# Sums of a graph network's SUM and REL rounds: one-hot products added to a resident accumulator, in place of scans, stored states and gathers

## The chip, the cores and the metric

One core of one Trainium2 chip runs the whole network in one launch. The metric is the time of one execution on the device in microseconds, lower is better.

## The reference

A network of 3125 nodes with 64 features and 103125 edges sorted by destination is computed in seven rounds over all edges. The two rounds that matter here, with layer norms between, are these (cut):

```python
# SUM
norm = deg_inv[from_] * deg_inv[to_]
out = segment_sum(norm[:, None] * x[from_], to_, n)
x = layernorm(x + out)
# two attention rounds (ATT) and a skip layer, then
# REL
transformed = einsum('nd,rdo->nro', h, weight)      # 16 relations
msg = transformed[src, rel_type] * norm             # norm = edge_weight1
x = layernorm(x + relu(segment_sum(msg, dst, n)))
# three edge convolutions with a segment maximum (MAX) follow
```

## The kernel before

The edges, padded, are cut into 808 tiles of 128 (P), and four tiles (TC) make a step: 202 steps in SUM, ATT and REL, 101 double steps in MAX. `ROUNDS` is SUM, ATT, ATT, REL, MAX, MAX, MAX. Each engine has its own instruction stream, and `chunks` writes a round's loop for it: a list of stages, each with a lag in steps, is run in that order for every step. A ring of U = 4 slots (2U in DVE's and SP's loop here) holds rows, indices and results. Semaphores of a round (`idx_ready`, `rows_ready`, `turned`, `st_ready`, `back`, `hb_ready`) count steps.

A step of SUM or REL runs like this. ACT copies four columns of source indices into `idx` (L1150; in SUM also four columns of node numbers, L1142). POOL issues four indirect gathers, each of 128 rows of 64 floats (L1086), into `rows` (shown as edges_a); it waits for `idx` and for `turned` of four steps before. In REL DVE multiplies the rows by the edges' weights (L1580). PE's `turn` (L1309) transposes the four tiles, so that features lie on partitions and 512 edges along the free axis. DVE's `scan` (L1562) runs along these 512 columns, from the value carried over of the last step: state = near x state + value, where `near` is 1 if an edge has the same destination as the one before it. PE's `back` (L1406) transposes the states again, ACT copies them out of PSUM (`states_out`, L1163, into hb) and stores them to DRAM (`store_states`, L1236, the table states_sum). The last edge of each node then holds that node's sum. SP fetches the near flags with `fetch_batch` (four steps at a time), in SUM also the destination numbers. SUM does more beside it, for later rounds: DVE makes one-hots of the destinations (`make_onehots`, L1569), SP stores them, PE turns the edge features (`turn_edges`, L1300), and ACT copies (`edges_back`, L1169) and SP stores them.

At the round's end POOL gathers the last state of every node, 25 gathers of 128 nodes (L1114), into `agg`, and the node phase goes over the nodes in six groups of four blocks and one last block: DVE's `scaled` in SUM (L822) or `related` in REL (L842) read `agg`, layer norms follow, PE turns the new x (L668) and multiplies it (L675), ACT and DVE split the products (L484 to L505), and SP stores the tables that the next round gathers from. The order of each engine's node steps is written out by hand (`STEPS`, `groups`).

Ahead of the rounds a preamble computes on DVE (L1439 to L1550) the degrees, block tables and the flags `tile_same` from the destinations of each tile (`tile_dst`), and SP stores the flags (L938, L940) and the first source table (L943). `first_i` holds each tile's first destination; ATT and MAX rounds load windows of 128 nodes from it (`fetch_windows`, L409 on).

## Time and profile before

| | us |
|---|---|
| median of 3 runs | 9922.08 |
| lowest, highest | 9895.71, 9936.42 |
| profiled execution, its span | 9918.4 |
| SUM: gathers from 64, last scan at 1282, ATT's gathers from about 1345 | |
| ATT, two rounds | about 1345 to 4560 |
| REL: gathers from 4722, last scan at 5927, MAX's gathers from 5980 | |
| MAX, three rounds | 5980 to about 9880 |

All times in the rows are of that one execution, counted from its span's start. PE is TensorE's matmul side, PEld its weight load, DVE VectorE, ACT ScalarE, POOL GpSimd, SP SyncE; SPq is SP's queue as it issues DMAs. "PEclk" is the granted TensorE clock as a share of 2.4 GHz. "<-" in square brackets names what ended an idle time; "remote" is a signal whose sender the profile does not name, "issue" is idle time with no wait that it shows.

### The profile page before, as it was taken

To read this page: it belongs to the slowest core of one execution; us is meant where nothing else is said; L and a number is where in the kernel's file an instruction comes from. 1 tells how busy PE (TensorE), PEld (TensorE's weight loads), DVE (VectorE), ACT (ScalarE), POOL (GpSimd) and SP (SyncE) were. 2 spreads that over 40 slices of the span, in tenths; PEclk is the share of its full clock that TensorE was granted. 3 is DMA by queue.
4 is the path that set the end of the run, shared out by engine and by line. 5 is a ranking of instruction groups with operands and counts; after the bars stand their busy time and mean duration, and the time that the engine had idled before them with its cause. 6 is when DMAs were issued, how large, how long until landed. Compare 5 with 4: busy or idle time off the path is not lost.

```text
span 9918.4 us, 123616 instructions
## 1 busy us (share of the span) xinstructions
PE 3937.1 (40%) x24024; PEld 2674.1 (27%) x24024; DVE 2471.0 (25%) x4351; ACT 2035.1 (21%) x6406; POOL 5554.5 (56%) x5874
## 2 busy tenths in 40 slices
PE   2333334443343433336222224444444444444443
PEld 1222223333342333334111112222222222222222
DVE  4333333333332333332222221111111111111112
ACT  1111123333332333333101111111111111111111
POOL 6666644454434444442666665666656666556665
PEclk9999995555555555555555555666656666566666
DMA  4444434454444444443222223333333333333333
GB/s 121 126 126 126 125 91 108 109 110 107 108 92 97 109 106 107 107 107 99 54 50 50 51 48 82 91 90 90 89 79 90 90 90 90 80 89 90 91 91 80
DMA packets 2188624, 925.94 MB, mean 93 GB/s; under 512 B 1608302, under 2 KB 2071734, under 8 KB 2182134
## 3 DMA queue, kind: packets, MB, share of 16 engines
q1 hardware_dynamic: 1080022, 458.65, 19.0%
q10 hardware_dynamic: 921120, 272.38, 11.7%
q0 software_dynamic: 187392, 193.93, 9.6%
q8 instruction: 30, 0.49, 0.0%
q14 instruction: 60, 0.49, 0.0%
HBM read 657.48 MB, written 266.58 MB: 93 GB/s over the span
## 4 chain that ended last, share of the span: by engine, by line
issue 30%; PE 20%; another core or an unknown queue 9%; SPq 7%; DVE 2%; DVEq 1%; ACT 1%; DMA 0%; ACTq 0%; POOL 0%; POOLq 0%
PE ps L1323 7%; PE ps L1398 5%; PE ps L1319 3%; SPq L1002 3%; PE ps L1406 2%; PE ps L675 1%; PE ps L1309 1%; DVEq L374 1%; SPq L996 1%; SPq L1004 1%; SPq L998 1%; DVE edges_a L1580 1%; DVE st L1562 0%; SPq L370 0%
## 5 line engine op out<-in xcount | busy, mean ns | idle before, releaser
L1086 POOL DMA_INDIRECT edges_a<-src_table,idx x4040 | 3829.6, 948 | 2501.2 <-issue 1163.6
L1093 POOL DMA_INDIRECT edges_a<-src_table,idx x1616 | 1524.7, 944 | 1626.7 <-ACT weighted L1209 1063.1
L1323 PE MATMUL ps<-sel,win_sb 128*64 128x128 fp8e4 x7272 | 749.7, 262 | 1704.9 <-issue 1703.6
L1562 DVE TENSOR_TENSOR_SCAN st<-pen,st,ps 128x512 f32<-128x512 f32 x300 | 384.0, 1280 | 3279.9 <-remote 2939.6
L1406 PE MATMUL ps<-ident,st 64*128 64x64 f32 (+2 forms) x4444 | 849.1, 339 | 655.0 <-DVE st L1562 333.8
L1406 PEld LDWEIGHTS ps<-ident,st 64*128 64x128 f32 (+2 forms) x4444 | 705.6, 207 | 1063.1 <-issue 1039.8
L1323 PEld LDWEIGHTS ps<-sel,win_sb 128*64 128x64 bf16 x7272 | 396.2, 126 | 2056.6 <-issue 2009.9
L1562 DVE TENSOR_TENSOR_SCAN st<-edges_a,st,ps 64x512 f32<-64x512 fp8e4 x402 | 510.5, 1270 | 1665.6 <-remote 1292.0
L1309 PE MATMUL ps<-ident,edges_a 128*64 128x128 f32 x1616 | 421.4, 416 | 985.2 <-DVE edges_a L1580 643.5
L1335 PE MATMUL ps<-win_sb,sel 128*128 128x97 bf16 x4848 | 473.8, 271 | 849.1 <-issue 771.5
L1163 ACT ACTIVATE hb<-ps 128x256 f32<-128x256 f32 (+1 forms) x808 | 348.4, 431 | 2000.1 <-remote 1082.1
L1390 PE MATMUL ps<-ident,weighted 128*97 128x128 f32 x1616 | 452.8, 433 | 615.9 <-issue 279.9
L1595 DVE TENSOR_TENSOR prod<-ps,edges_a 128x388 f32<-128x388 f32 x404 | 225.4, 558 | 1795.3 <-remote 1459.7
L1335 PEld LDWEIGHTS ps<-win_sb,sel 128*128 128x128 fp8e4 x4848 | 396.1, 135 | 909.9 <-issue 826.0
L1319 PE MATMUL ps<-ident,edges_a 128*128 128x128 f32 x1212 | 439.2, 362 | 425.3 <-issue 354.7
L1227 ACT ACTIVATE edges_a<-ps,b 128x512 f32<-128x512 f32 x303 | 208.2, 687 | 1658.0 <-remote 1498.9
L1390 PEld LDWEIGHTS ps<-ident,weighted 128*97 128x97 f32 x1616 | 337.5, 274 | 659.9 <-issue 640.2
L1562 DVE TENSOR_TENSOR_SCAN st<-decay,st,ps 97x512 f32<-97x512 f32 x402 | 511.5, 1272 | 10.4 <-PE ps L1406 10.4
L1309 PEld LDWEIGHTS ps<-ident,edges_a 128*64 128x64 f32 x1616 | 216.4, 158 | 1063.7 <-issue 996.2
L1161 ACT ACTIVATE hb<-ps 128x512 f32<-128x512 f32 x303 | 180.9, 597 | 1555.4 <-issue 1386.1
L1398 PE MATMUL ps<-edges_a,w 128*128 128x512 f32 x606 | 481.9, 887 | 9.7 <-issue 8.0
L1209 ACT ACTIVATE weighted<-edges_a,weight 128x97 f32<-128x97 f32 x1616 | 471.9, 364 | 33.3 <-ACT hb L1163 23.9
(203 smaller groups left out, 3440.4 us busy)
## 6 DMA issues: line engine op xcount, KB each, us to landing
states_sum<-hb ACTq DMA_DIRECT2D x1010, 128.0 KB
win_sb<-dst_table SPq DMA_DIRECT2D x1616, 72.8 KB
edges_a<-src_table,idx POOLq DMA_INDIRECT x5656
states_att<-hb ACTq DMA_DIRECT2D x404, 194.0 KB
win_sb<-dst_table ACTq DMA_DIRECT2D x1212, 48.0 KB
win_sb<-dst_table SPq DMA_DIRECT2D x1212, 48.0 KB
dst_b<-in_dst_row SPq DMA_DIRECT2D x50, 1024.0 KB
sel<-onehots SPq DMA_DIRECT2D x303, 128.0 KB
```

The costliest lines, as they stand in the source:

```text
L1086: pool.indirect_dma_start(rows[:, s, j * D:(j + 1) * D], None, srcs[q.r], bass.IndirectOffsetOnAxis(ap=idx[:, s, j:j + 1], axis=0))\
L1093: pool.indirect_dma_start(xe_a[:, s, j * KA:j * KA + D], None, srcs[q.r], bass.IndirectOffsetOnAxis(ap=idx_a[:, s, j:j + 1], axis=0))\
L1163: nc.scalar.activation(hb[:, v, 0:TC * kw], bank(BACK, s)[:, 0:TC * kw], ACT.Copy)\
L1209: last = nc.scalar.activation(weighted[:, s % V, j * KA:(j + 1) * KA], xe_a[:, s, j * KA:(j + 1) * KA], ACT.Copy, scale=weight[:, gs_, o + ...
L1309: last = nc.tensor.matmul(bank(TURNED, s)[0:D, j * P:(j + 1) * P], rows[:, s, j * D:(j + 1) * D], ident[:, :], is_transpose=True, start=Tr ...
L1319: nc.tensor.matmul(bank(TURNED, s)[:, at_j], rows[:, s, j * P:(j + 1) * P], ident[:, :], is_transpose=True, start=True, stop=False)
L1323: last = nc.tensor.matmul(bank(TURNED, s)[h * D:h * D + D, at_j], win_pair(s, j, h)[:, i * D:(i + 1) * D], sel[:, s, h * EC + j * P:h * EC ...
L1335: last = nc.tensor.matmul(bank(TURNED, s)[:, j * KA:(j + 1) * KA], sel[:, v, j * P:(j + 1) * P], win_att(v, j)[:, i * KA:(i + 1) * KA], st ...
L1390: last = nc.tensor.matmul(bank(QUERY, s)[0:KA, j * P:(j + 1) * P], weighted[:, s % V, j * KA:(j + 1) * KA], ident[:, :], is_transpose=True ...
L1398: nc.tensor.matmul(bank(QUERY, s), w2[:, q.r - 4, :], xe[:, s, :], start=True, stop=True).then_inc(q.lifted.sem, 1)
L1406: last = nc.tensor.matmul(bank(BACK, s)[:, j * w:(j + 1) * w], st[0:w, s % V, j * P:(j + 1) * P], ident[0:w, 0:w], is_transpose=True, star ...
L1562: nc.vector.tensor_tensor_scan(st[0:w, s % V, :], d0, d1, init, op0, op1).then_inc(q.st_ready.sem, 1)
```

## The change

Rounds of the kinds in `WINDOWED`, SUM and REL, no longer scan, transpose back, store or gather states. As the destinations are sorted, the 128 edges of a tile reach into a window of at most 128 nodes, from the tile's first destination on. `slot`, made once in the preamble, holds for every edge its destination less the first one of its tile. In each step DVE makes one-hots `xe` from it (`spread_edges`: in SUM one instruction for four tiles, in REL four that carry the edge's weight as well and replace L1580); PE multiplies rows by one-hots (`window_sums`: four plain float32 matmuls of 128 columns in place of four transposes) into PSUM; and one step later DVE adds the four windows of 64 x 128 into a resident accumulator `acc` of 64 x 3328 at the column that a register gives (`add_windows`). POOL's gathers wait for `summed` in place of `turned`. In the node phase PE transposes `acc` by groups (`turn_sums`, after the last add), and `scaled` and `related` read PSUM in place of `agg`; POOL's 25 gathers are left out there. ACT's `states_out` and `store_states`, SP's near flags of SUM and all of SP's fetches of REL go. The one-hots and the edge features of SUM stay. The preamble gets seven transposes, three DVE instructions and an iota for `slot` and `ramp` (0 to 127), and SP clears two stretches of 6144 rows of the state table that MAX reads, ahead of the flags' stores. `acc` is `agg` under another name, `slot` is the former `mask`.

```diff
+WINDOWED = (SUM, REL)
...
-    self.turned = shared("turned", C_)
-    self.st_ready = shared("st_ready", C_)
-    self.back = shared("back", C_)
-    self.hb_ready = shared("hb_ready", C_)
-    if kind in (SUM, REL):
-        self.batch_ready = [shared(f"batch_ready_{h}", 16 * (1 + (kind == SUM)) * len(range(h * U, C, 2 * U)))
-                            for h in range(2)]
+    if kind in WINDOWED:
+        self.spread = shared("spread", C_)
+        self.summed = shared("summed", C_)
+        self.added = shared("added", TC * C_)
+    else:
+        self.turned = shared("turned", C_)
+        self.st_ready = shared("st_ready", C_)
+        self.back = shared("back", C_)
+        self.hb_ready = shared("hb_ready", C_)
     if kind == SUM:
+        self.batch_ready = [shared(f"batch_ready_{h}", 16 * len(range(h * U, C, 2 * U))) for h in range(2)]
         self.sel_made = shared("sel_made", C_)
         self.nodes_ready = shared("nodes_ready", C_)
-    if kind == REL:
-        self.weighted = shared("weighted", C_)
...
+def turn_sums(g):
+    b, nb = GROUPS[g]
+    wait(pe, (q.added, TC * q.steps))
+    if g >= V:
+        wait(pe, dve_did(q, g - V, "scaled" if r == 0 else "added"))
+    for j in range(nb):
+        last = nc.tensor.matmul(bank(SCORE, g)[:, j * D:(j + 1) * D], acc[0:D, (b + j) * P:(b + j + 1) * P],
+                                ident[0:D, 0:D], is_transpose=True, start=True, stop=True)
+    last.then_inc(q.pe.sem, 1)
...
-    dve.wait_ge(agg_ready[g], 16 * nb * (r + 1))
-    op(g, "scaled", nc.vector.tensor_tensor(y, a_g, wide(dinv[:, b:b + nb], D), ALU.mult))
+    wait(dve, pe_did(q, g, "turn_sums"))
+    op(g, "scaled", nc.vector.tensor_tensor(y, blocks_of(bank(SCORE, g), nb, D), wide(dinv[:, b:b + nb], D), ALU.mult))
...
+for end in (CH * EC, EP):
+    sp.dma_start(states[0][end - LATE_CHUNKS * EC:end, :].rearrange("(p n) f -> p n f", p=P),
+                 zrow[:, :].bitcast(f32)[:, 0:D].unsqueeze(1).to_broadcast([P, LATE_CHUNKS * TC, D]))\
+        .then_inc(tails_cleared, 16)
...
-        if k == SUM:
-            wait(sp, (q.sel_made, c - U))
-            e = slice(c * EC, (c + m) * EC) if isinstance(c, int) else bass.ds(c * EC, m * EC)
-            sp.dma_start(dst_b[:, of_slots, :].rearrange("p u e -> p (u e)"),
-                         dst_row[:, e].to_broadcast([P, m * EC])).then_inc(q.batch_ready[h].sem, 16)
-        wait(sp, (q.st_ready, c - U))
-        sp.dma_start(near[:, of_slots, :].bitcast(u8).rearrange("p u e -> p (u e)"),
-                     flags[of, :].rearrange("(o u) e -> o (u e)", o=1).to_broadcast([D, m * EC]))\
-            .then_inc(q.batch_ready[h].sem, 16)
+        wait(sp, (q.sel_made, c - U))
+        e = slice(c * EC, (c + m) * EC) if isinstance(c, int) else bass.ds(c * EC, m * EC)
+        sp.dma_start(dst_b[:, of_slots, :].rearrange("p u e -> p (u e)"),
+                     dst_row[:, e].to_broadcast([P, m * EC])).then_inc(q.batch_ready[h].sem, 16)
...
-        wait(sp, *tables_stored(q))
+        if k != REL:
+            wait(sp, *tables_stored(q))
-    elif k == REL:
-        chunks(sp, q.steps, (0, fetch_batch), ring=2 * U)
...
-        wait(pool, *sources_stored(q), (q.idx_ready, c + 1), (q.turned, c - U + 1))
+        wait(pool, *sources_stored(q), (q.idx_ready, c + 1),
+             (q.summed if q.kind in WINDOWED else q.turned, c - U + 1))
...
+    if q.kind in WINDOWED:
+        continue
...
-        chunks(act, q.steps, (0, indices), *[(U, edges_back)] * (k == SUM), (U + 1, states_out),
-               (U + 2, store_states))
+        chunks(act, q.steps, (0, indices), *[(U, edges_back)] * (k == SUM))
...
-    def turn(c, s, n):
-        made = [(q.weighted, c + 1)] if k == REL else []
-        wait(pe, (q.rows_ready[s], 64 * (n + 1)), *made, (q.st_ready, c - V + 1))
+    def window_sums(c, s, n):
+        wait(pe, (q.rows_ready[s], 64 * (n + 1)), (q.spread, c + 1), (q.added, TC * (c - U + 1)))
         for j in range(TC):
-            last = nc.tensor.matmul(bank(TURNED, s)[0:D, j * P:(j + 1) * P], rows[:, s, j * D:(j + 1) * D],
-                                    ident[:, :], is_transpose=True, start=True, stop=True)
-        last.then_inc(q.turned.sem, 1)
+            at_j = slice(j * P, (j + 1) * P)
+            last = nc.tensor.matmul(window_ps(s)[:, at_j], rows[:, s, j * D:(j + 1) * D], xe[:, s, at_j],
+                                    start=True, stop=True)
+        last.then_inc(q.summed.sem, 1)
...
-        chunks(pe, q.steps, *[(0, turn_edges)] * (k == SUM), (0, turn), (1, back))
+        chunks(pe, q.steps, *[(0, turn_edges)] * (k == SUM), (0, window_sums))
...
+for m, b in ((P, slice(0, whole)), (T - whole * P, slice(whole, whole + 1))):
+    nc.vector.tensor_tensor(tile_slot[0:m, b, :], tile_dst[0:m, b, :],
+                            tile_dst[0:m, b, 0:1].to_broadcast([m, b.stop - b.start, P]), ALU.subtract)\
+        .then_inc(slots_made, 1)
...
+dve.wait_ge(slots_turned, 1)
+nc.vector.tensor_copy(slot[:, :], slot_ps[:, 0:T]).then_inc(slots_set, 1)
+dve.wait_ge(ramp_set, 1)
+dve.wait_ge(slots_set, 1)
...
-        wait(dve, (q.batch_ready[h], 32 * (n + 1)), (q.nodes_ready, c + 1), (sel_stored[h], 16 * n))
+        wait(dve, (q.batch_ready[h], 16 * (n + 1)), (q.nodes_ready, c + 1), (sel_stored[h], 16 * n))
...
-    def step_plain(c, s, n):
+    def scan_pair(c, s, n):
+        wait(dve, (q.lifted, c + 1), (q.pen_ready, c + 1))
+        scan(c, s, pen[:, s % V, :], bank(QUERY, s), ALU.add, ALU.max)
+    def spread_edges(c, s, n):
+        wait(dve, (q.summed, c - U + 1))
         if k == SUM:
-            make_onehots(c, s, n)
-        if k == REL:
-            wait(dve, (q.rows_ready[s % U], 64 * (2 * n + s // U + 1)))
-            weighted = rows[:, s % U, 0:TC * D].rearrange("p (j f) -> p j f", f=D)
-            nc.vector.tensor_tensor(weighted, weighted,
-                                    wgt_sb[:, cols(c, TC)].unsqueeze(2).to_broadcast([P, TC, D]),
-                                    ALU.mult).then_inc(q.weighted.sem, 1)
-            wait(dve, (q.batch_ready[s // U], 16 * (n + 1)))
-        if k == MAX:
-            wait(dve, (q.lifted, c + 1), (q.pen_ready, c + 1))
-            scan(c, s, pen[:, s % V, :], bank(QUERY, s), ALU.add, ALU.max)
-        else:
-            wait(dve, (q.turned, c + 1))
-            scan(c, s, near[:, s, :], bank(TURNED, s)[0:D, :], ALU.mult, ALU.add)
+            nc.vector.tensor_tensor(xe[:, s % U, :].rearrange("p (j e) -> p j e", e=P),
+                                    ramp[:, :].unsqueeze(1).to_broadcast([P, TC, P]),
+                                    slot[:, cols(c, TC)].unsqueeze(2).to_broadcast([P, TC, P]),
+                                    ALU.is_equal).then_inc(q.spread.sem, 1)
+            return
+        for j in range(TC):
+            at = cols(c * TC + j)
+            last = nc.vector.tensor_scalar(xe[:, s % U, j * P:(j + 1) * P], ramp[:, :], slot[:, at], wgt_sb[:, at],
+                                           ALU.is_equal, ALU.mult)
+        last.then_inc(q.spread.sem, 1)
+    def add_windows(c, s, n):
+        _, begins = nc.values_load_multi_w_load_instructions(
+            first_i[0:1, cols(c, TC)], engines=[mybir.EngineType.DVE],
+            skip_runtime_bounds_check_because="setup puts every edge's node in [0, N] and pads with N")
+        wait(dve, (q.summed, c + 1))
+        for j in range(TC):
+            window = acc[0:D, bass.ds(begins[j], P)]
+            wait(dve, (q.added, TC * c + j))
+            nc.vector.tensor_tensor(window, window, window_ps(s % U)[:, j * P:(j + 1) * P], ALU.add)\
+                .then_inc(q.added.sem, 1)
...
+    elif k == MAX:
+        chunks(dve, q.steps, (0, scan_pair))
     else:
-        chunks(dve, q.steps, (0, step_plain), ring=U if k == MAX else 2 * U)
+        nc.vector.memset(acc[0:D, :], 0.0).then_inc(sums_cleared, 1)
+        dve.wait_ge(sums_cleared, 1 if k == SUM else 2)
+        chunks(dve, q.steps, *[(0, make_onehots)] * (k == SUM), (0, spread_edges), (1, add_windows),
+               ring=2 * U if k == SUM else U)
...
```

## Rows read from the trace of the kernel before

**Rows 1.** The page, part 1: busy time, share of the span, instructions.

```profile
PE 3937.1 (40%) x24024; PEld 2674.1 (27%) x24024; DVE 2471.0 (25%) x4351; ACT 2035.1 (21%) x6406; POOL 5554.5 (56%) x5874
```

**Rows 2.** Stretches of 200 us, busy (instructions) of PE, PEld, DVE, ACT, POOL; PEclk.

```profile
1000.00:1200.00 200.00, 72.73 (x396) 50.65 (x396) 67.99 (x166) 32.72 (x135) 126.12 (x133) 1.00 0.50 129
5000.00:5200.00 200.00, 56.10 (x272) 35.18 (x272) 54.00 (x68) 19.55 (x67) 129.77 (x137) 0.50 0.22 49
```

**Rows 3.** Timeline of POOL in REL: start, us, instruction [idle before it].

```profile
5385.53 0.94 POOL L1086 DMA_INDIRECT edges_a<-src_table,idx  x1 [3.65 <-remote]
...
5404.34 0.94 POOL L1086 DMA_INDIRECT edges_a<-src_table,idx  x1 [0.30 <-issue]
5408.83 0.94 POOL L1086 DMA_INDIRECT edges_a<-src_table,idx  x1 [3.54 <-remote]
```

**Rows 4.** Timeline of DVE in the same stretch of REL.

```profile
5395.00 1.27 DVE L1562 TENSOR_TENSOR_SCAN st<-edges_a,st,ps 64x512 f32<-64x512 fp8e4 x1 [2.55 <-issue]
5396.20 0.39 DVE L1580 TENSOR_TENSOR edges_a<-edges_a,wgt_sb 128x256 f32<-128x256 f32 x1
5408.14 1.27 DVE L1562 TENSOR_TENSOR_SCAN st<-edges_a,st,ps 64x512 f32<-64x512 fp8e4 x1 [11.55 <-remote]
```

**Rows 5.** Timeline of PE in the same stretch of REL.

```profile
5396.85 1.03 PE L1309 MATMUL ps<-ident,edges_a 128*64 128x128 f32 x4 [2.49 <-DVE st L1562]
5397.81 0.69 PE L1406 MATMUL ps<-ident,st 64*128 64x64 f32 x4
5410.07 1.03 PE L1309 MATMUL ps<-ident,edges_a 128*64 128x128 f32 x4 [11.57 <-DVE edges_a L1580]
```

**Rows 6.** Waits from 200 to 1200 us, SUM: us in total, times, longest.

```profile
POOL edges_a L1086 <- remote: 128.8, 43, 3.8
...
POOL edges_a L1086 <- ACT idx L1150: 42.5, 20, 5.4
```

**Rows 7.** Waits from 4800 to 5800 us, REL.

```profile
POOL edges_a L1086 <- remote: 138.2, 51, 4.3
...
POOL edges_a L1086 <- ACT idx L1150: 18.9, 6, 5.5
```

**Rows 8.** Timeline of DVE in SUM, a catch-up.

```profile
914.53 1.26 DVE L1562 TENSOR_TENSOR_SCAN st<-edges_a,st,ps 64x512 f32<-64x512 fp8e4 x1
915.72 0.85 DVE L1569 TENSOR_SCALAR sel<-dst_b,nodes 128x128 fp8e4<-128x128 int32 x4
916.58 1.27 DVE L1562 TENSOR_TENSOR_SCAN st<-edges_a,st,ps 64x512 f32<-64x512 fp8e4 x1
```

**Rows 9.** Timeline of DVE in the preamble: widths and forms.

```profile
47.56 0.43 DVE L1467 TENSOR_SCALAR joint<-node_id,first_f,before_f 128x25 f32<-128x25 f32 x1
...
52.09 0.68 DVE L1445 TENSOR_TENSOR agg<-agg,node_id 128x512 f32<-128x512 int32 x1
...
53.72 0.29 DVE L1445 TENSOR_TENSOR agg<-agg,node_id 128x128 f32<-128x128 int32 x1
```

**Rows 10.** Timeline of SP's queue in an ATT round.

```profile
2007.73 0.01 SPq L996 DMA_DIRECT2D sel<-onehots  x1
2008.52 1.88 SPq L1002 DMA_DIRECT2D win_sb<-dst_table  x4
```

**Rows 11.** Timeline of PE in SUM's node phase: plain float32 matmuls.

```profile
1304.51 2.02 PE L675 MATMUL ps<-wquery,xT 65*128 65x97 f32 x8 [0.68 <-issue]
```

**Rows 12.** Timeline of SUM's end and node phase, all engines.

```profile
1287.60 0.94 POOL L1114 DMA_INDIRECT agg<-states_sum,last_i  x1 [14.29 <-DMA states_sum<-hb]
...
1293.76 0.42 DVE L822 TENSOR_TENSOR gy<-agg,dinv 128x256 f32<-128x256 f32 x1 [10.35 <-DMA agg<-states_sum,last_i]
1293.84 1.16 POOL L1114 DMA_INDIRECT agg<-states_sum,last_i  x1 [0.30 <-issue]
...
1322.89 0.56 DVE L498 TENSOR_TENSOR split_r<-ps,split 128x388 f32<-128x388 f32 x1 [5.44 <-ACT split L484]
```

**Rows 13.** Timeline of DVE at REL's end.

```profile
5928.12 0.39 DVE L842 SCALAR_TENSOR_TENSOR gy<-agg,xn 128x256 f32<-128x256 f32 x1
```

More of the change, by code:

```diff
@@ L121, in gnn_kernel @@
         mask = sb("mask", [P, T])
+        slot = mask
+        ramp = sb("ramp", [P, P])
         tiles_le = sb("tiles_le", [P, NB])
@@ L167, in gnn_kernel @@
         tile_same = sb("tile_same", [P, TB, P], f8)
-        near = edges_a[0:D, U * EC:U * EC + U * EC // 2].bitcast(f8)\
-            .rearrange("p (u e) -> p u e", u=2 * U)
         pen = sb("pen", [P, V, EC])
@@ L202, in gnn_kernel, with window_ps @@
         TURNED, QUERY, SCORE, BACK = range(4)
+        def window_ps(s):
+            return ps[0:D, U + s, :]
         chain_ps = ps[:, 4, :]
@@ L220, in gnn_kernel @@
         flags_stored = sem("flags_stored")
+        ramp_set = sem("ramp_set")
+        slots_made = sem("slots_made")
+        slots_turned = sem("slots_turned")
+        slots_set = sem("slots_set")
+        sums_cleared = sem("sums_cleared")
         pens_made = sem("pens_made")
@@ L351, in __init__ @@
                 self.per_step = 2 if kind == MAX else 1
-                self.st_stored = [shared(f"st_stored_{s_}", 16 * self.per_step * uses[s_]) for s_ in range(U)]
+                self.gathered = sum(k not in WINDOWED for k in ROUNDS[:r + 1])
+                self.st_stored = [] if kind in WINDOWED else [shared(f"st_stored_{s_}", 16 * self.per_step * uses[s_])
+                                                              for s_ in range(U)]
                 self.src_stored = [sem(f"src_stored_{r}_{s_}") for s_ in range(V if kind == REL else 1)]
@@ L466, in gnn_kernel @@
         LATE = 3
+        LATE_CHUNKS = 12
         PRE_EDGES = 2 + NB + 5 * G + 10
@@ L840, in related @@
                 b, nb, u, y, xc, sq, x_g, z_g, a_g = of_group(g)
-                dve.wait_ge(agg_ready[g], 16 * nb * (r + 1))
-                op(g, "added", nc.vector.scalar_tensor_tensor(y, a_g, 0.0, x_g, ALU.max, ALU.add))
+                wait(dve, pe_did(q, g, "turn_sums"))
+                op(g, "added", nc.vector.scalar_tensor_tensor(y, blocks_of(bank(SCORE, g), nb, D), 0.0, x_g, ALU.max, ALU.add))
                 statistics(g)
@@ L1290, in _ @@
             last.then_inc(ids_turned, 1)
+            pe.wait_ge(slots_made, 2)
+            for b in range(TB):
+                w = min(P, T - b * P)
+                last = nc.tensor.matmul(slot_ps[:, b * P:b * P + w], tile_slot[0:w, b, :], ident[0:w, 0:w],
+                                        is_transpose=True, start=True, stop=True)
+            last.then_inc(slots_turned, 1)
             for q in rounds:
```

30 lines of the change are left out of this document (18 added, 12 removed).

## The prediction

> **What bounds the kernel now.** I read the busy shares first. POOL, which does little but issue the indirect gathers, leads with 56% [rows 1]; no engine is full, so the bound must be a pace or a wait, read round by round. The 200 us stretches give it [rows 2]: in the SUM round POOL issues 133 gathers in 200 us, in the REL round 137. Each round has 202 steps of four gathers (808), so SUM takes 808 x 200/133 = 1215 us (6.01 us a step) and REL 808 x 200/137 = 1180 us (5.84 us a step). DVE is busy a third of that and PE less than 40%.
>
> Next the POOL timeline of REL [rows 3]. One gather takes 0.94 us, and sixteen starts lie 18.81 us apart (5385.53 to 5404.34), 1.25 us each, so four cost 5.0 us; the rest of a step is pauses. They are regular: sixteen gathers back to back (5385.53 to 5405.28), then 3.54 us idle, released by "remote", and again. From one resumption to the next 23.3 us pass, 5.83 us a step: the pace measured. The floor, gathers with no pause, is 808 x 1.25 = 1010 us a round: 205 us under SUM and 170 us under REL.
>
> Who ends the pause? DVE weighs the rows of a step at 5396.20 [rows 4], PE turns them at 5396.85 and is through at 5397.88 [rows 5], yet the scan that waits for this turn starts at 5408.14, after 11.55 us idle, and POOL goes on at 5408.83. So PE's result was ten microseconds old before DVE and POOL saw it, and they saw it only when POOL had paused. Then things go quickly: the next turn, of rows that had waited 11.57 us for DVE, runs at 5410.07. In the waits of 1000 us the same thing is POOL's 128.8 us for "remote" in SUM [rows 6] and 138.2 us in REL [rows 7]. I call it the late signal. It is a reading of this trace, and why it is late is not visible. The round is thus a cycle: POOL gathers until its ring of four is exhausted, stops some 3.4 us, the signal comes, and the other engines catch up in a fast stretch of about 10 us until it is late again. **What counts is how many steps a cycle releases:** three give (15.0 + 3.4)/3 = 6.13 us a step, four 5.85, five 5.68.
>
> **Part by part.**
>
> *DVE.* Removed: the scan, 1.27 us a step, and in REL the weighing, 0.39 [rows 4]. In SUM scan and one-hots repeat every 2.05 us [rows 8], in REL a step of the catch-up takes 3 us, because weigh, turn and scan are in series. Added: the spread. In SUM it is one 128x512 TENSOR_TENSOR, the form that took 0.68 us [rows 9]. In REL it is four 128x128 TENSOR_SCALARs with two pointers: no row shows one; below it lies 0.29 us of a 128x128 TENSOR_TENSOR, above it 0.43 us, which two pointers cost on 25 columns [rows 9], plus the 103 columns more (0.13 us, from 0.68 - 0.29 for 384). Four are 1.2 to 2.2 us; I take 1.5, nearer the row of the same size. Added too: four 64x128 adds, each waiting for the one before it. One is 0.29 us by the same row, and at most doubled by its wait and register address, which no row shows: 1.2 to 2.4, I take 1.9. Then a load of four registers; SP does such a load ahead of its window fetches and needs 0.79 us from one DMA to the next (2007.73 to 2008.52) [rows 10]. I take 0.5 of bounds 0.1 to 0.8. With SUM's four one-hots (0.85 us [rows 8]) a step is 0.85 + 0.7 + 0.5 + 1.9 = 3.95 us, bounds 2.9 to 4.8, in SUM and 1.5 + 0.5 + 1.9 = 3.9, bounds 2.5 to 5.4, in REL. Both lie below POOL's 5.0, but a catch-up step is now no faster than 3.9 us, where it was 2.05 and 3.0.
>
> *PE.* Removed: turn (1.03) and back (0.69) [rows 5]. Added: four plain float32 products of 128 columns; four of 97 columns took 2.02 us [rows 11], so 2.0 to 2.7 us, taken 2.1. PE stays below 45% busy. POOL is now released by an operation of 2.1 instead of 1.03 us, but a late signal hides that.
>
> *The order.* Here the change helps. Spread comes one step ahead of add, so when DVE hangs in the add of step k, the spread of k+1 is made, and PE can multiply k+1 while the signal of k is late; before, DVE had to scan k before REL's rows of k+1 were weighed. At time 0 of the fast stretch k and k+1 are both seen. Then in REL add k ends at 2.4 (load included), spread k+2 at 3.9, its product at 6.0; add k+1 at 6.3, spread k+3 at 7.8, product at 9.9. The old catch-up that began with POOL's resumption at 5385.53 ran its fourth scan at 5395.00 [rows 4], 9.5 us on. So the fourth step comes in at about the same time, the cycle stays at four, and **REL stays at 5.85 a step, +2 us**. In SUM the one-hots add 0.85 - 0.8 = 0.05 to the DVE step and the turned edges 0.6 to PE: the fourth product ends at about 10.5, so a cycle takes four steps or three, 5.85 or 6.13. I take half each, 5.99: **SUM -4 us**.
>
> *ACT and SP.* ACT's copies and 404 stores of states go, and so do SP's near flags. ACT's idx(c) stood behind them on its queue, and POOL waited for idx 42.5 us in 1000 in SUM [rows 6] and 18.9 in REL [rows 7]: 52 and 22 us a round. In SUM idx still stands behind edges_back, which itself waits for PE's late signal. The late product ends the same pauses, so I count a third: **-17 and -7 us**, bounds 0 and -74 together. The DMA traffic that goes lies beside the gathers and is worth nothing by itself.
>
> *Node phases.* SUM: the first aggregate gather starts at 1287.60 after 14.29 us for the states' landing, and the first L822 at 1293.76, 10.35 us after the last scan's end [rows 12]. Instead there will be an add (2.4), a turn of four blocks (1.06, as L668) and some 0.5: -6 us. The 25 gathers go, and with them the late signals among them, of which the largest is the 5.44 us ahead of L498 [rows 12]; I count two of that size: -11. **Together -17 us.** REL: L842 starts at 5928.12, right behind the last scan [rows 13], since its gathers had begun before. An add and a turn in between cost 3.5 us, and one late stretch of 5 us may go: **0 us**, bounds -5 and +5.
>
> *Preamble.* DVE gets a subtraction of 128x768 (0.68 x 1.5 = 1.0 us by [rows 9]), one of 40x128 (0.3) and one copy of 128x808 (0.6 to 2.3): +2 us. Two clears of 6144 rows of 256 B stand on SP's queue ahead of the flags and of the first source table. The queue issues nothing else for some 15 us there, about what they need; **+3 us in all**, bounds 0 and +15. MAX and ATT are untouched.
>
> **The sum.** Against the profiled execution's own 9918.4 us: +2 - 4 - 17 - 7 - 17 + 0 + 3 = -40. Its span is 3.7 us under the median of the three runs, which lie 41 us apart; carried over, 9922 - 40 = **9,882 us**.
>
> **The rivals.**
>
> *The pauses shrink.* If adds and spreads are at their low ends (DVE 2.5 to 2.9 us a step), a fifth step fits into the fast stretch: 5.68 in both rounds, -67 and -32 us, with the node phases 9,785 us. If the late signal goes altogether, because two steps of slack cover it, both rounds come down to the floor: -205 - 170 - 14 = 9,533 us. For it speaks that PE no longer waits for a fresh result of DVE. Against it: aggregate gathers alone, with few other DMAs beside them, show late signals too (the 5.44 us of [rows 12]), so it comes with the gathers, and these remain.
>
> *DVE becomes the clock (the slower side).* If each dependent add takes 0.6 us or more and the load 0.8, a catch-up step in either round is over 4.6 us, the fourth step falls out of the fast stretch and often the third: 6.13 in REL (+60) and 6.13 to 6.9 in SUM (+24 to +180). With -17 - 24 + 3 that is 9,965 to 10,120 us, and I price it at 10,020. It decides from a DVE step of some 4.4 us; that DVE is busy only a third of the time now [rows 2] is no help, since the catch-up counts.
>
> *The shared port.* A gather runs 0.94 us alone, and 1.16 us at 1293.84 [rows 12] beside a 0.42 us TENSOR_TENSOR of two SBUF inputs, +0.22. With a spread in every step, at most four such hits in REL and one or two in SUM, less the weighing's own: 202 x (0.66 + 0.2) = +170 us if all fall under gathers, but the pauses absorb part of it: 9,990 us. The Trainium skill ("SBUF — State Buffer", section "Who interferes with whom") says that a tensor_scalar in a two-port mode and a GpSimd operation block each other for the whole instruction, and that a tensor_tensor with both inputs in SBUF contends only with GpSimd's reads; the 1.16 us row shows a contention of that kind. By that rule it would be REL's four TENSOR_SCALARs that block most.
>
> *Only the node phases move*: cycles as before, ACT's waits replaced by PE's: 9,922 - 17 + 3 = 9,908 us.
>
> **How the numbers follow.** Forecast (9,840 to 9,930): 0.36, of which 0.12 lies over 0.5% below the median. Shrunken pauses (9,533 to 9,840): 0.28. DVE as the clock: 0.22. The port: 0.05. Node phases alone: 0.09. 0.5%, or 50 us, is about what a measurement of this kernel can tell from no change. Faster: 0.12 + 0.28 = 0.40. Slower: 0.22 + 0.05 = 0.27. Same: 0.24 + 0.09 = 0.33. Since the rivals of both signs hold half the chance, the range is 9,640 to 10,060, leaving out 0.1 on each side; the forecast's own is 9,840 to 9,930.
>
> **What would show it.** In the profile after: gathers per 200 us (133 and 137 if right, 150 or more without pauses, 125 or fewer if DVE is the clock); pauses of 3.4 us after sixteen gathers; DVE's time from one spread to the next in a fast stretch (3.9 us) and the length of an add (0.3 us, pitch under 0.5); no POOL wait for idx in REL; L822 about 4 us behind the last add; gathers longer than 1.0 us beside spreads. The prediction is wrong if the late signal is not a property of the gathers but of what was removed, or if the adds are dearer than 0.6 us each.

## The result and the profile after

The changed kernel takes 10,301.6 us (median of four runs, 10,280 to 10,323) against 9,908.9 us of the kernel before in the same session: **4.07% slower, ratio 1.0407 with a 95% interval of 1.039 to 1.0424**. The forecast was 9,882 us with a range that ended at 10,060. The profiled execution has a span of 10,278.5 us, 360 us over that of before. The first and the last gather of each round in the two traces say where they are:

| us | before | after | difference |
|---|---|---|---|
| SUM, first to last gather | 1208 | 1342 | +134 |
| from there to ATT's first | 72 | 65 | -7 |
| ATT and the relation table | 3377 | 3359 | -18 |
| REL, first to last gather | 1180 | 1457 | +277 |
| from there to MAX's first | 78 | 74 | -4 |
| MAX | 3871 | 3850 | -21 |

All of the loss lies in the two rounds that were changed, and twice as much in REL. The page, with busy time, share and instructions, and its lines of the gathers and of the new adds:

```profile
PE 4067.7 (40%) x24081; PEld 2896.4 (28%) x24081; DVE 2721.7 (26%) x6377; ACT 1881.3 (18%) x6002; POOL 5530.2 (54%) x5825
...
L1113 POOL DMA_INDIRECT edges_a<-src_table,idx x4040 | 3848.8, 953 | 2900.2 <-issue 1182.0
...
L1645 DVE TENSOR_TENSOR agg<-agg,ps 64x128 f32 x1616 | 452.1, 280 | 1675.0 <-issue 1202.9
```

DVE has 2026 instructions more than in [rows 1], POOL is as busy as before, and a gather is as long (953 against 948 ns over all rounds). The adds are short, 280 ns, but idle time stands ahead of them. The stretches of 200 us, one in SUM and one in REL, to be laid beside [rows 2]:

```profile
core 0: us, PE busy (x) PEld busy (x) DVE busy (x) ACT busy (x) POOL busy (x), PEclk, DMA share, GB/s
1000.00:1200.00 200.00, 74.95 (x362) 61.94 (x360) 77.87 (x271) 17.56 (x90) 116.08 (x119) 1.00 0.33 86
5400.00:5600.00 200.00, 54.45 (x225) 43.87 (x224) 63.69 (x225) 5.75 (x28) 105.37 (x112) 0.50 0.10 18
```

SUM went from 133 to 119 gathers, REL from 137 to 112. Over the whole rounds a step takes 6.65 us (5.99 before) and 7.22 us (5.85). PEclk is as before, 1.00 and 0.50. One cycle of REL on the timeline, as in [rows 3 to 5] (start, duration, engine, instruction, idle time before it):

```profile
5313.36 1.11 DVE L1632 TENSOR_SCALAR edges_a<-ramp,mask,wgt_sb 128x128 f32<-128x128 f32 x4 [0.44 <-issue]
...
5314.76 1.94 PE L1344 MATMUL ps<-edges_a 128*64 128x128 f32 x8 [2.90 <-DVE edges_a L1632]
5315.05 0.28 DVE L1645 TENSOR_TENSOR agg<-agg,ps 64x128 f32 x1 [0.58 <-issue]
...
5318.14 0.28 DVE L1645 TENSOR_TENSOR agg<-agg,ps 64x128 f32 x1 [2.81 <-issue]
...
5321.87 0.95 POOL L1113 DMA_INDIRECT edges_a<-src_table,idx  x1 [0.30 <-issue]
5323.68 0.28 DVE L1645 TENSOR_TENSOR agg<-agg,ps 64x128 f32 x1 [5.26 <-issue]
...
5325.52 0.28 DVE L1645 TENSOR_TENSOR agg<-agg,ps 64x128 f32 x1 [1.55 <-issue]
5325.84 1.11 DVE L1632 TENSOR_SCALAR edges_a<-ramp,mask,wgt_sb 128x128 f32<-128x128 f32 x4
...
5327.21 1.94 PE L1344 MATMUL ps<-edges_a 128*64 128x128 f32 x8 [10.51 <-DVE edges_a L1632]
5327.51 0.28 DVE L1645 TENSOR_TENSOR agg<-agg,ps 64x128 f32 x1 [0.55 <-issue]
5328.33 0.28 DVE L1645 TENSOR_TENSOR agg<-agg,ps 64x128 f32 x1 [0.55 <-DVE agg L1645]
5329.15 0.28 DVE L1645 TENSOR_TENSOR agg<-agg,ps 64x128 f32 x1 [0.54 <-DVE agg L1645]
5329.92 0.95 POOL L1113 DMA_INDIRECT edges_a<-src_table,idx  x1 [7.11 <-PE ps L1344]
```

POOL's twelve gathers began at 5308.11; the twelfth starts at 5321.87, and it goes on at 5329.92, after 7.11 us idle. 21.8 us for three steps are 7.27 us a step. The product that releases it (5327.21) had waited 10.51 us for its spread (5325.84). The spread stood behind the four adds of the step before on DVE's queue: 5315.05, 5318.14, 5323.68, 5325.52. The second and third of these, 0.28 us each, came 3.1 and 5.5 us after the one before; a few microseconds on, with POOL idle, the adds of the next step follow each other every 0.82 us. Between the late adds DVE ran control instructions: those that its sequencer handles alone, here waits for semaphores, register arithmetic and bounds checks. The chain of work through this stretch shows them (start, duration, what; L386 and L390 are the helpers for waits, "q" is DVE's own sequencer):

```profile
by line: issue 38.2%; DVEq L1645 24.2%; DVE agg L1645 11.1%; DVEq L390 7.6%; DVE edges_a L1632 7.1%; DVEq L386 6.8%; DVEq L1638 2.9%; DVEq L1632 2.2%; DVEq L417 0.3%
...
5315.86 0.70 DVEq L386
5316.56 0.71 DVEq L390
...
5318.14 0.28 DVE agg L1645
...
5318.70 0.70 DVEq L1645
...
5320.83 0.70 DVEq L386
5321.54 0.69 DVEq L390
...
5322.93 0.70 DVEq L1645
5323.68 0.28 DVE agg L1645
```

**DVE gets through one control instruction per 0.70 us here.** Twelve of them follow on the first add until 5325.03: seven last 0.70 us, the other five 0.02 us or less, with five idle pieces of the same 0.70 us between them ("issue"). A few microseconds earlier the same kinds take 0.02 to 0.19 us. The first long one came 7.7 us after POOL resumed; the last ended at 5325.03, 2.2 us after its last gather. Over all of REL the medians are 7.1 and 2.1 us, and 53 of 60 cycles have three steps; before, 39 of 46 had four. In the waits of 1000 us in REL (total, times, longest):

```profile
PE ps L1344 <- DVE edges_a L1632: 635.1, 102, 12.9
DVE agg L1645 <- issue: 539.9, 319, 10.2
POOL edges_a L1113 <- PE ps L1344: 321.3, 45, 9.3
...
DVE agg L1645 <- DVE agg L1645: 125.8, 229, 0.9
```

POOL lost 321 us to the product (138.2 us to "remote" in [rows 7]), the product 635 us to the spread, and DVE 540 us to its own issue.

SUM has something more. The page's line of the queue that loads instructions (packets, MB, share) is, before and then after:

```profile
q14 instruction: 60, 0.49, 0.0%
q14 instruction: 178, 1.46, 0.0%
```

Of the 178 packets 122 start in SUM (4 of 60 before) and 3 in REL. DVE's loop of SUM holds eight steps of 29 control instructions and the work itself, and at each of its 23 branches DVE now stands still, 5.5 us at the median and 107 us in all, where it was 0.11 us before. In REL the same branch costs 0.23 us. One such place in SUM (the branch ends at 238.86, the next control instruction starts at 241.89, and two of these packets start in between):

```profile
242.29 0.87 DVE L1613 TENSOR_SCALAR sel<-dst_b,nodes 128x128 fp8e4<-128x128 int32 x4 [3.32 <-issue]
```

### The profile page after: what moved, and what is told of

It is laid out like the page before. It is cut to its first block, busy times and chain, and to the rows that moved or that the text cites. A ratio compares the mean times of both kernels' runs of the same rounds, so it can differ in the third digit from the quotient of the medians.

```text
span 10278.5 us, 132298 instructions
## 1 busy us (share of the span) xinstructions
PE 4067.7 (40%) x24081; PEld 2896.4 (28%) x24081; DVE 2721.7 (26%) x6377; ACT 1881.3 (18%) x6002; POOL 5530.2 (54%) x5825
## 4 chain that ended last, share of the span: by engine, by line
issue 43%; PE 18%; SPq 15%; DVEq 11%; DVE 7%; another core or an unknown queue 3%; DMA 1%; ACT 1%; ACTq 0%; POOL 0%; POOLq 0%
SPq L1028 7%; DVEq L1645 7%; PE ps L1358 7%; PE ps L1433 4%; PE ps L1354 3%; DVE agg L1645 3%; PE ps L1441 2%; SPq L1030 2%; SPq L1022 2%; DVEq L390 2%; SPq L1024 2%; DVE edges_a L1632 1%; DVE sel L1613 1%; DVEq L386 1%
## 5 line engine op out<-in xcount | busy, mean ns | idle before, releaser
L1344 PE MATMUL ps<-edges_a 128*64 128x128 f32 x3232 | 783.5, 424 | 1927.9 <-DVE edges_a L1632 919.1
L1344 PEld LDWEIGHTS ps<-edges_a 128*64 128x64 f32 x3232 | 633.2, 224 | 2025.5 <-issue 2000.6
L1645 DVE TENSOR_TENSOR agg<-agg,ps 64x128 f32 x1616 | 452.1, 280 | 1675.0 <-issue 1202.9
L1441 PE MATMUL ps<-ident,st 97*128 97x97 f32 (+1 forms) x2828 | 573.5, 348 | 26.8 <-issue 21.6
L1441 PEld LDWEIGHTS ps<-ident,st 97*128 97x128 f32 (+1 forms) x2828 | 502.6, 204 | 279.1 <-issue 268.3
L1248 ACT ACTIVATE decay<-sel 97x508 f32<-97x508 fp8e4 x404 | 249.8, 618 | 669.6 <-DVE st L1606 446.4
```

The lines of the kernel that those rows point to most:

```text
L1344: last = nc.tensor.matmul(window_ps(s)[:, at_j], rows[:, s, j * D:(j + 1) * D], xe[:, s, at_j], start=True, stop=True)
L1441: last = nc.tensor.matmul(bank(BACK, s)[:, j * w:(j + 1) * w], st[0:w, s % V, j * P:(j + 1) * P], ident[0:w, 0:w], is_transpose=True, star ...
L1645: nc.vector.tensor_tensor(window, window, window_ps(s % U)[:, j * P:(j + 1) * P], ALU.add)\
```

## The experiments

Theory A: the loss comes from the control instructions that the change gives DVE, because they are long while gathers run back to back. Counted on DVE's queue in the traces (waits, register arithmetic and bounds checks, without loads and branches), REL has 7 a step before and 32 after, SUM 5 and 29. The earlier expectations below say 34. Theory B: PE's plain products, 1.94 us against 1.03 us of transposes, release POOL later.

**The first four kernels ran on another chip, and there the kernel before takes 7,647 us (16 runs), not 9,900.** Of the edits below, those with one add or with adds at fixed places and the transposes leave out that the sums land at their nodes; one window per step computes everything.

```diff
 # e1_one_add: one add of all four windows at a fixed place
-    for j in range(TC):
-        window = acc[0:D, bass.ds(begins[j], P)]
-        wait(dve, (q.added, TC * c + j))
-        nc.vector.tensor_tensor(window, window, window_ps(s % U)[:, j * P:(j + 1) * P], ALU.add)
+    wait(dve, (q.summed, c + 1), (q.added, c))
+    window = acc[0:D, 0:EC]
+    nc.vector.tensor_tensor(window, window, window_ps(s % U), ALU.add)
 # e3_fixed_windows: four adds, four waits, no registers
-        window = acc[0:D, bass.ds(begins[j], P)]
+        window = acc[0:D, j * P:(j + 1) * P]
 # e4_transposes: on PE
-        nc.tensor.matmul(window_ps(s)[:, at_j], rows[:, s, j * D:(j + 1) * D], xe[:, s, at_j], start=True, stop=True)
+        nc.tensor.matmul(window_ps(s)[:, at_j], rows[:, s, j * D:(j + 1) * D], ident[:, :], is_transpose=True, ...)
 # e2_step_window: slot counted from the step's first tile, one window
-        nc.tensor.matmul(window_ps(s)[:, at_j], ..., start=True, stop=True)
+        nc.tensor.matmul(window_ps(s)[:, 0:P], ..., start=j == 0, stop=j == TC - 1)
+    window = acc[0:D, bass.ds(begins[0], P)]
+    nc.vector.tensor_tensor(window, window, window_ps(s % U)[:, 0:P], ALU.add)
```

> The changed kernel, but the four adds of a step (each with its register address and its wait) become one 64x512 add at a fixed place, without a register load; what is left out is that the sums land at their nodes. Theory A (DVE's control instructions: 34 a step in the changed kernel against 7 before, each 0.7 us long while gathers run): the instructions fall to about 12 a step, the spread is no longer late, REL returns to 5.7 to 5.9 us a step and SUM to 5.8 to 6.1, total 9,820 to 9,920 us. Theory B (PE's plain products of 1.94 us in place of 1.03 us of transposes release POOL later): nothing changes, 10,230 us or more.

> The changed kernel with its four adds and their four waits, but at fixed columns: no register load, no address arithmetic, no bounds checks; what is left out is that the sums land at their nodes. Theory A: some 16 control instructions a step less, half the loss goes, about 10,050 to 10,120 us, REL 6.3 to 6.6 us a step. If the dependence between the adds alone were the cause (a chain of four results), it stays above 10,250 us. Theory B: stays above 10,250 us.

> The changed kernel, but PE transposes the four tiles (1.03 us) in place of the four plain products (1.94 us); spread and adds stay as they are. The sums are left out. Theory A: no more than 0.9 us per cycle of three steps comes back, 60 us a round at the very most and more likely half of it in all, 10,200 to 10,290 us. Theory B: the whole loss goes, 9,900 to 9,950 us.

> A version that computes everything: one window per step. slot is counted from the first destination of the step's first tile (two more DVE operations in the preamble), PE accumulates the four products in one PSUM window of 64x128, and DVE makes one add with one loaded register. Theory A: about 13 to 15 control instructions a step on DVE, REL 5.7 to 6.0 us a step, SUM 5.8 to 6.1; total 9,830 to 9,940 us, level with the kernel before or up to 0.8% faster. Theory B: 10,230 us or more.

Measured against 7,646.9 us: one add 7,718 (ratio 1.0092, 1.0072 to 1.0112), fixed windows 7,655 (1.0009, 0.9999 to 1.0019), transposes 7,678 (1.0041, 1.0026 to 1.0057), one window per step 7,674 (1.0036, 1.0022 to 1.005). None of the numbers expected was near, for either theory, because they were made for the first kind of chip. Two stretches of the kernel with transposes, SUM and REL (columns as above):

```profile
800.00:1000.00 200.00, 58.99 (x296) 38.26 (x296) 99.09 (x346) 22.63 (x112) 153.07 (x155) 1.00 0.45 116
3600.00:3800.00 200.00, 41.35 (x160) 21.47 (x160) 89.25 (x320) 8.21 (x40) 151.24 (x161) 0.50 0.14 26
```

155 and 161 gathers in 200 us: POOL runs at its floor of 1.25 us in REL (5.00 us a step), with DVE's adds, registers and checks all there. What is different shows in DVE's queue at the adds' line: count, and min/median/max in ns, on this chip and then in the changed kernel's REL on the first one:

```profile
L1645 DVEq FUSED_REGOPS  x1279: 46/190/190, 3502.1 to 4299.8; - x183
L1645 DVEq SEQ_ASSERT  x1278: 23/23/23, 3502.3 to 4299.4; - x183
```

```profile
L1645 DVEq FUSED_REGOPS  x1426: 1/53/1400, 4900.5 to 6200.0; - x179
L1645 DVEq SEQ_ASSERT  x1426: 1/23/1403, 4900.7 to 6200.0; - x179
```

The same bounds check takes 23 ns each time here and up to 1403 ns there. So the long control instructions belong to the chip or its surroundings together with this kernel, not to the code alone. All later kernels ran on four other chips, where the kernel before takes 9,909 to 9,931 us (medians), and each is compared with the kernel before on its own chip.

> The changed kernel itself, beside the kernel before. The first four runs took place where the kernel before needs 7,647 us and where none of their traces has a control instruction of 0.7 us. Theory A says that the loss of 4.1% needs those long control instructions: where the kernel before takes 7,650 us, the changed one is within 1% of it (7,600 to 7,720 us), with POOL at 1.25 us a gather in REL; where the kernel before takes 9,900 us, it takes 10,300 us again. Theory B (PE's longer products): slower by 4% at either place.

> One 64x512 add at a fixed place in place of the four adds, as in the first run of this edit; the sums don't land at their nodes. Theory A: at a place where the kernel before takes 9,900 us, 9,820 to 9,920 us; where it takes 7,650 us, within 1% of the changed kernel. Theory B: 10,230 us or more at the first kind of place.

The changed kernel again: 10,314 us, ratio 1.0393 (1.0366 to 1.042). One add: **9,825.8 us, ratio 0.9902** (0.9878 to 0.9926), as theory A had it. PE's products are in it unchanged, so theory B can't hold: the whole loss hangs on the adds with what stands around them. (Its page has 58 packets of the instruction queue, so what SUM loses by loading is gone in it too.)

> PE transposes the four tiles (1.03 us) in place of the four plain products (1.94 us); spread and adds as in the changed kernel; the sums are left out. At a place where the kernel before takes 9,900 us. Theory A: 10,200 to 10,310 us, the loss stays. Theory B (longer products release POOL later): 9,900 to 9,950 us.

> The version that computes everything with one window, one accumulated PSUM tile and one add per step. At a place where the kernel before takes 9,900 us. Theory A: 14 control instructions a step on DVE against 34, so 9,840 to 9,960 us, a little above the one add at a fixed place (9,826 us), which has 8. Theory B: 10,230 us or more.

> Four adds and four waits at fixed columns, without register load, address arithmetic and bounds checks; the sums don't land at their nodes. At a place where the kernel before takes 9,900 us. Theory A: 16 control instructions a step, 9,880 to 10,050 us. If it is the chain of four dependent adds that costs, 10,250 us or more.

> The kernel before, with the one wait for turned ahead of DVE's scan in SUM and REL written nine times: 16 more control instructions a step on DVE (23 in REL), in a kernel that has none of the change's adds. At a place where the kernel before takes 9,900 us. Theory A, if control instructions cost wherever they stand on DVE: slower by 1 to 4%, 10,020 to 10,300 us. If only the adds or the products matter: within 0.5% of the kernel before. Where the kernel before takes 7,650 us: within 0.5% by every theory.

```diff
 # b2_before_waits, in the kernel before
+    for _ in range(8):
         wait(dve, (q.turned, c + 1))
     scan(c, s, near[:, s, :], bank(TURNED, s)[0:D, :], ALU.mult, ALU.add)
```

Transposes: 10,394 us, 1.0497 (1.0471 to 1.0522). Theory B is refuted a second time; theory A's number was missed too, by 80 us on the other side (10,310 was its upper end). SUM took 7.45 us a step and REL 7.07:

```profile
800.00:1000.00 200.00, 43.92 (x220) 28.45 (x220) 70.57 (x244) 16.42 (x84) 104.99 (x110) 1.00 0.31 81
5200.00:5400.00 200.00, 29.45 (x115) 15.03 (x113) 63.17 (x225) 5.75 (x28) 108.81 (x115) 0.50 0.10 19
```

PE is busy 44 and 29 us of 200, and POOL is slower still in SUM. Why a shorter product makes SUM slower stays open: control instructions (29 a step), loading (122 packets, 111 us at the branches) and granted clock (1.00) are as in the changed kernel. Fixed windows: 9,850.8 us, 0.9946 (0.9933 to 0.9958), better than expected: four dependent adds and four waits cost next to nothing once registers and checks are gone. Yet REL has as many control instructions of 0.65 to 0.75 us in it, 449, as in the changed kernel, 448. How many are long doesn't decide, then, but how many DVE has to get through before the next spread. Waits repeated in the kernel before: 9,975 us, 1.0073 (1.0049 to 1.0097), the right way and less than expected; the trace shows why, a repeated wait is one control instruction, not two, so there were 7 more a step in REL, where a step went from 5.85 to 6.17 us, in a kernel without anything of the change. **One window per step: 9,834.3 us, 0.9931 (0.9911 to 0.995)**, everything computed:

```profile
800.00:1000.00 200.00, 78.89 (x408) 65.57 (x408) 60.65 (x210) 22.39 (x104) 134.09 (x135) 0.54 0.38 98
5200.00:5400.00 200.00, 64.92 (x280) 53.27 (x280) 51.96 (x180) 6.84 (x34) 130.37 (x137) 0.53 0.12 22
```

In SUM its granted clock is 0.54, where the slower changed kernel has 1.00: TensorE's clock isn't what holds the round back. In REL 31 of 40 cycles have five steps.

Next, whether the number of control instructions alone does it, and whether it takes gathers back to back.

```diff
 # b3_dose (10) and b4_dose_full (20), in the version with one window per step
     wait(dve, (q.summed, c + 1), (q.added, c))
+    for _ in range(20):
+        wait(dve, (q.added, c))
 # b3_spaced, b3_spaced_before, b4_step_spaced: POOL, SUM and REL
+    wait(pool, (q.spaced, TC * c))
     for j in range(q.per_step * TC):
         pool.indirect_dma_start(...)
+        pool.memset(prod[:, j * 97:j * 97 + 96], 0.0).then_inc(q.spaced.sem, 1)
```

> The version with one window and one add per step, with its wait for added repeated ten times ahead of the add: 34 control instructions a step on DVE, as many as the changed kernel has, but one add, one register and no chain of adds. At a place where the kernel before takes 9,900 us. Theory A (their number costs): 10,150 to 10,350 us. If it is the four adds or their addresses: within 0.5% of the version without the repeats, 9,790 to 9,880 us.

> The changed kernel, with a small memset on POOL after each gather of SUM and REL, so that gathers start some 1.5 us apart in place of 1.25. At a place where the kernel before takes 9,900 us. If the long control instructions come with gathers back to back at 1.25 us, they become few and POOL's pauses vanish: SUM and REL take 6.0 to 6.4 us a step in place of 6.65 and 7.21, total 9,950 to 10,150 us. If they don't depend on the gathers' spacing, each gather's 0.25 us is added or hidden in the pauses: 10,300 to 10,450 us.

> The kernel before with the same memset after each gather of SUM and REL. At a place where the kernel before takes 9,900 us. If gathers back to back cause the late signals, the pauses vanish and the pace is the spaced gathers' own, 6.0 to 6.4 us a step against 5.99 and 5.84: 9,910 to 10,080 us, with POOL's pauses below 1 us a step. If they don't, the pauses stay and the time rises by 0.25 us a gather: 10,250 us or more.

> The version with one window and one add per step, the wait for added repeated twenty times: about 32 control instructions a step on DVE in REL, like the changed kernel, but one add. At a place where the kernel before takes 9,900 us. If their number alone makes the loss: REL at 6.9 to 7.4 us a step, total 10,200 to 10,350 us. If register addresses or the chain of adds are needed for it: REL below 6.5 us a step, 9,960 to 10,100 us.

> The version with one window, with one small memset on POOL after the fourth gather of each step of SUM and REL, for which the next step's gathers wait: 5.6 us a step if nothing else holds POOL. If gathers this far apart keep the control instructions short: both rounds at 5.6 to 5.7 us a step in place of 5.90 and 5.82, total 9,740 to 9,790 us. If the long ones still come: pauses on top of the memset, 9,840 us or more.

> The version with one window, with a memset after each gather of SUM and REL: 5.85 to 5.93 us a step, as the spaced kernels showed. Expected within 0.3% of the version without memsets (9,810 to 9,860 us) and with no long control instruction on DVE in REL.

The doses: 9,970 us with 22 a step (1.006, 1.0042 to 1.0077), 10,154.7 us with 32 (1.0227, 1.0202 to 1.0253). The first was expected to be a dose of 34, 10,150 us or more; as each repeat is one instruction, it was a smaller dose. The second fell between its two expected ranges in total, with REL, at 6.90, just in the range for their number alone. The second, SUM and REL:

```profile
800.00:1000.00 200.00, 80.16 (x386) 66.22 (x385) 57.07 (x192) 18.76 (x96) 123.87 (x128) 0.50 0.37 94
5200.00:5400.00 200.00, 55.57 (x230) 45.20 (x231) 39.71 (x140) 5.75 (x28) 106.73 (x114) 0.50 0.10 19
```

Laid in order, all on the kind of chip where before takes 9,900 us:

| kernel | DVE's control instructions a step in REL | REL, us a step | SUM, us a step | total, us |
|---|---|---|---|---|
| one add, fixed place | 8 | 5.76 | 5.88 | 9,826 |
| one window per step | 12 | 5.82 | 5.90 | 9,834 |
| four adds, fixed places | 15 | 5.84 | 5.94 | 9,851 |
| one window, waits x11 | 22 | 6.15 | 6.02 | 9,970 |
| one window, waits x21 | 32 | 6.90 | 6.27 | 10,155 |
| the changed kernel | 32 | 7.22 | 6.65 | 10,302 |
| the changed kernel, transposes on PE | 32 | 7.07 | 7.45 | 10,394 |
| the kernel before | 7 | 5.85 | 5.99 | 9,909 |
| the kernel before, waits x9 | 13 | 6.17 | 6.02 | 9,975 |

Up to 15 they are hidden, from 22 on they are not. At 32 their number alone accounts for 3.0 of the 4.8 per cent between the version with one window (0.9931) and the changed kernel (1.0407), since the repeats bring it to 1.0227. By rounds (first to last gather) that is 218 of REL's 283 us and 75 of SUM's 152. REL's other 65 us go with the three further adds, which the runs don't divide between their 0.28 us, their place between the control instructions and their registers. SUM's other 77 us go with these and with the loading of instructions: the kernel of 32 by repeated waits has 63 packets on that queue and 0.23 us at its branches, so it lacks both, and no run divides them. In the kernel before, where scan, turn and weighing stand in series, seven more already show.

The spacing. The spaced changed kernel took **9,931.8 us, ratio 1.002** (1.0008 to 1.0031), 370 us less than the changed kernel, although only work and a wait for POOL were added. One boundary of a step on POOL, and the stretch of REL:

```profile
5259.51 0.20 POOL L1121 MEMSET prod<- 128x96 f32 x1
5259.87 0.95 POOL L1117 DMA_INDIRECT edges_a<-src_table,idx  x1 [0.16 <-issue]
5260.82 0.19 POOL L1121 MEMSET prod<- 128x96 f32 x1
5261.77 0.95 POOL L1117 DMA_INDIRECT edges_a<-src_table,idx  x1 [0.75 <-issue]
```

```profile
5200.00:5400.00 200.00, 65.27 (x270) 53.02 (x271) 75.49 (x270) 6.98 (x34) 154.78 (x269) 0.50 0.12 22
```

(269 counts gathers and memsets.) Gathers mostly start 1.30 us apart in a step and 1.90 us at its boundary, with longer ones 5.9 us a step. In REL's 6544 control instructions none is of the 0.7 us kind (448 in the changed kernel). POOL's pauses (starts over 2.2 us apart, less 1.25 us each) fall from 444 us in sum to 12. In SUM the cure is partial: 243 long ones are left of 286, with 6.23 us a step in place of 6.65 and, as in the changed kernel, 122 packets of loading. The expectation had 9,950 to 10,150 us. The kernel before with the same spacing took 9,912.6 us, ratio 1.0003 (0.9992 to 1.0013): its pauses went too (164 to 12 us in REL), and the time into the spacing. With one window per step, four memsets gave 9,885 us (0.9958, 0.9937 to 0.998), a little more than expected, and one memset, after the fourth gather only (b4_step_light), 9,857 us (0.9933, 0.9911 to 0.9958), not the 9,740 to 9,790 expected. Its total lies in the range given for long ones that still come, but they don't: in its REL 8 control instructions are long, against 265 without memset, and a step takes 5.79 us. The memset with its wait, and 29 us of pauses, take up what the others lost. So spacing gives the changed kernel back nearly all that it lost, and gains nothing where the control instructions are few.

## Why the prediction was wrong

*The late signal* was read rightly as something that comes while gathers run and ends when POOL pauses: the spaced runs show it. It belongs to the gathers and not to the stores, which the changed kernel's REL no longer has. What was missed is that in such a stretch DVE itself is slow. In the trace of after it gets through one control instruction per 0.70 us, and the step of the working that failed is **"DVE", which priced adds, load and spread as busy time plus a doubled wait and asked only whether a catch-up step stays under POOL's 5.0 us**. It took no account of how many control instructions an add at a register's column brings (REL went from 7 a step to 32), nor that a bounds check of 0.02 us is 30 times as long in a slow stretch. Four adds and what stands between them took 10 us there, where 1.9 us were priced.

In the kernel before the same stretches look different. Only 3 of REL's control instructions last 0.65 to 0.75 us. Instead DVE's queue shows nothing from 5395.37 to 5403.85, and then a wait of 4.15 us that ends at 5408.10, both for results of PE that were ready by 5398.50; the medians over REL's cycles are 8.0 and 4.5 us. That both are one cause is likely, since spacing the gathers removes POOL's pauses in either kernel, but it isn't shown.

*The sizes.* A 128x128 spread of REL was 1.11 us for four (taken 1.5, below my lower bound of 1.2), SUM's 0.68 (taken 0.7), an add 0.28 us (0.29) but 0.82 us from one to the next even in a fast stretch, four in 3.3 us against 1.9 taken and 2.4 as the bound (at fixed columns it is 0.38 us). The prediction had named "dearer than 0.6 us each" as a sign of being wrong. PE's four products took 1.94 us (taken 2.1). The register load (0.34 us) runs beside the spread. A catch-up step of REL is therefore 4.4 to 4.8 us, not 3.9.

*The order* did not help as I had it. Spread one step ahead of add means that the spread of step k+2 stands behind the adds of k. When these take 10 us, the product waits for it, and POOL's pause in REL grows from 3.6 to 7.5 us on the mean. "The cycle stays at four" failed with it: cycles went to three steps, as the rival had it, but not at (15.0 + 3.4)/3 = 6.13.

*The rival "DVE becomes the clock"* named the right engine and the right side. Its threshold, a catch-up step of some 4.4 us, was passed (4.4 to 4.8 measured), but it isn't what decides. The kernel with 32 control instructions by repeated waits spreads every 3.8 us when it catches up, below even the forecast's 3.9, and still falls to three steps in 52 of 61 cycles:

```profile
5217.03 1.11 DVE L1639 TENSOR_SCALAR edges_a<-ramp,mask,wgt_sb 128x128 f32<-128x128 f32 x4 [0.43 <-issue]
...
5220.86 1.12 DVE L1639 TENSOR_SCALAR edges_a<-ramp,mask,wgt_sb 128x128 f32<-128x128 f32 x4
```

What DVE gets done while the gathers run decides. The rival's price, 10,020 us and at most 10,120, was made with pauses of 3.4 us and is 180 us short at its most. Its chance of 0.22 was too low for a change that more than quadruples an engine's sequencer instructions.

*The shared port* did not decide: gathers average 949 ns in REL, where the four TENSOR_SCALARs stand, against 953 before. In SUM they average 977 against 957, 16 us in all.

*ACT and SP, node phases*: POOL's wait for idx is gone from REL and stands at 1.8 us in 1000 in SUM, as forecast. The node phases moved as forecast where they are counted as the prediction did, from the last scan or add to the next round's gathers: SUM's from 61 to 43 us (-17 forecast), REL's from 52 to 54 (0). But in SUM the last add ends 22 us after the last gather, where the last scan ended after 11, so from gather to gather only 7 us are gained, and 4 in REL. In the version with one window it is 20 and 19 us. The preamble cost nothing: the first gather starts at 64 us in both (+3 forecast).

## What to carry to other kernels

Count the sequencer instructions that an edit gives an engine (register loads, address arithmetic, bounds checks, waits), not only its busy time, and look in the trace at how long such instructions take in the stretch where the edit will stand. Where operations with run-time addresses can be merged ahead of the address (here: accumulate four products in one PSUM window and add once), the same algorithm goes from 4% slower to 0.7% faster. That holds for the chips at 9,900 us; on the one at 7,647 us this version is 0.4% slower than the kernel before, so such a gain is to be measured on more than one chip. Look also at the instruction queue's packets when an edit lengthens an unrolled loop: here they rose from 60 to 178, with 5.5 us lost at each branch of one loop. A kernel that is bound by one engine's back-to-back requests may be helped by spacing these, if the pauses that they cause are longer than the spacing.

## What the runs showed of the hardware that was not expected

The same kernel before takes 7,647 us on one chip and about 9,910 us on others, four of them in the later runs. In REL gathers (0.95 us), adds (0.28 us) and products (1.94 us) are as long in the kernels traced on either; what differs is the pauses, and in the traces of the slower chips control instructions of 0.7 us, which come some 7 us after gathers 1.25 us apart set in, and end about 2 us after they stop. With gathers at 5.9 us a step none came in REL.

It is not DVE's alone. In the changed kernel's REL only DVE's are long, while ACT's and POOL's in the same stretch stay short. But in SUM of the kernel before, 337 of ACT's 2450 instructions that are not counted as busy and 567 of SP's 2095 last 0.65 to 0.75 us, and 2 of DVE's 1063; none of POOL's do.

What makes them long, and why one chip has them and the other not, no run here settles. The loading of instructions isn't it in REL: the changed kernel has 3 packets of it there against 448 long control instructions. The changed kernel itself was not run on the faster chip; the nearest to it there is the one with transposes.
